# A recommendation tower (embedding look-up, pairwise products, three dense layers): the last chunk gets an order of its own, and its last gathered row another bank

## The chip, the cores and the metric

The kernel runs on one core of a Trainium2 chip. The metric is the device time of one launch in microseconds (us). TensorE multiplies matrices (PE in the rows, PEld for its weight loads), ScalarE (ACT) and VectorE (DVE) move and transform data, GpSimd (POOL) issues the indirect gathers, and SyncE (SP) issues the other DMAs. SBUF is the on-chip memory, PSUM the memory that TensorE writes, in banks of 512 float32 per partition.

## The reference, cut to what matters

```python
e = stack([tbl_f[ids[:, f]] for f in range(26)], axis=1)      # 2048 x 26 x 128
combined = concatenate([dense[:, None, :], e], axis=1)        # 2048 x 27 x 128
interactions = einsum('bnd,bmd->bnm', combined, combined)
z = concatenate([dense, interactions[:, triu_i, triu_j]], 1)  # 128 + 351
h = concatenate([z, dense], axis=1)                           # 607
h = maximum(h @ W_top1 + b_top1, 0)                           # 512
h = maximum(h @ W_top2 + b_top2, 0)                           # 256
y = h @ W_top3                                                # 2048 x 1
```

All values are float32. For each of 2048 samples 26 table rows are looked up, the 351 products of pairs among 27 vectors are made, and a small network follows.

## The kernel before, in words

The samples go in 8 chunks of 256 (chunk 0 to 7, `LAST` = 7), each of two tiles of 128. Of the 26 tables, 9 are looked up by one-hot matmuls from SBUF (`look_up`, line 446), and 17 are gathered row by row with one indirect DMA per table and tile (`gather`, lines 396 to 406, on GpSimd's queue). The gathered rows of a tile come in five batches of 4, 4, 4, 4 and 1 tables. `turn(t, b)` (lines 418 to 430) transposes batch b of tile t on TensorE into the one PSUM bank `moved`; ScalarE's `keep_batch` (827) copies it into `vectors` and counts `batch_kept`. As `moved` is one bank, every `turn` waits until the batch before it has been copied (line 426).

When the 27 vectors of a tile are there, `multiply(c, s)` (452 to 472) makes the products of step s of chunk c. A step is 64 samples, in two visits of 32 samples; each sample is one small matmul of 27 by 27, which the profile shows as two matmul records and two weight loads. Step s writes bank s of `banks`. Steps 0 and 1 are the first tile, steps 2 and 3 the second. `keep_step` (844 on ScalarE, 706 on VectorE for the very last step) copies the bank to `products`, and `write_quad` (217) writes them to a scratch tensor in HBM, three DMAs for each of four groups of partitions; one DMA loads them back as `features`, so that pairs lie on partitions. Then come `first_layer` (474, four output tiles m), `second_layer` (493, two output tiles) and `last_layer` (504), always of the chunk before: in chunk i the layers of chunk i-1 are mixed in among the products.

The order of each engine is written out by hand. On TensorE `chunk(i)` (625) does the first tile's batches and look-ups and ends with `end_of_chunk(i)` (639): first layers of the chunk before, steps 0 and 1, the five batches of the second tile, second layers, and, where there is a next chunk, steps 2 and 3 between its first look-up. For the last chunk `end_of_chunk` stops after batch 4, and `end()` (565) takes over: step 2 in two visits with halves of `second_layer(6, 1)` between, step 3 whole, and then the last chunk's own layers. These are done in two halves of 128 samples: `first_of_half(0, m)`, m 0 to 3 (line 535), `second_of_half(0)` (549), the dense part of `first_of_half(1, m)`, `last_of_half(0)` (560), the rest of `first_of_half(1, m)`, `second_of_half(1)`, `last_of_half(1)`. `last_layer(6)` stands between m = 1 and m = 2 of half 0.

On SyncE the end is `write_last(0)` (301; 12 DMAs, after step 1 is copied), `load_last(0)` (309; after these have landed), `write_last(1)` (six DMAs, after step 3 is copied; ScalarE issues the other six), `store_y(6)` (292; after chunk 6's y is copied), `load_last(1)` (after both sets of six have landed) and the stores of y. VectorE ends with `end()` (734): `keep_second` for chunk 6, `keep_step(7, 3)`, and the copies of half 0's layers with `keep_y` among them.

Of the kernel before, what the change touches and what calls it, by code (L numbers as in the profile page):

```python
# [20 lines left out]
TILE = 128  # L21
# [3 lines left out]
ALL_TILES = CHUNKS * TILES  # L25
LAST = CHUNKS - 1
# [39 lines left out]
assert CHUNK_STEPS == BANKS  # L66
KINDS = [ROWS[SHORT_] // PART_ROWS for SHORT_ in (ONE_HOT[0], ONE_HOT[-1])]
# [40 lines left out]
def build(nc, dense, ids, ids_of_field, tables, w1, b1, w2, b2, w3, out):  # L108
# [6 lines left out]
    with ExitStack() as ctx:  # L115
# [301 lines left out]
        def _(pe):  # L417
            def turn(t, b):
# [6 lines left out]
                if n:  # L425
                    pe.wait_ge(batch_kept, n)
                for m, v in enumerate(batch):
                    last = nc.tensor.transpose(moved[:, m * TILE:(m + 1) * TILE],  # L428
                                               rows[:, (t * TILE_ROWS + v) % RING, :], identity[:, :])
# [22 lines left out]
            def multiply(c, s, visits=range(VISITS)):  # L452
                for visit in visits:
                    multiply_part(c, s, visit)
# [110 lines left out]
            def end():  # L565

                every = (PAIR_TILES, *range(PAIR_TILES))
                multiply(LAST, 2, (0,))
                second_layer(LAST - 1, 1, range(0, 2))
                multiply(LAST, 2, (1,))  # L570
                second_layer(LAST - 1, 1, range(2, MTILES1))
                multiply(LAST, 3)
                first_of_half(0, 0, every)
                first_of_half(0, 1, every)
                last_layer(LAST - 1)
# [49 lines left out]
            def chunk(i):  # L625
# [11 lines left out]
                end_of_chunk(i)  # L637

            def end_of_chunk(i):
# [15 lines left out]
                if i < LAST:  # L655
                    second_layer(i - 1, 1)
                    multiply(i, 2, (0,))
                    look_up(i + 1, 0, range(0, 3))
                    multiply(i, 2, (1,))
                    look_up(i + 1, 0, range(3, 5))  # L660
                    multiply(i, 3, (0,))
                    look_up(i + 1, 0, range(5, PARTS[0]))
                    multiply(i, 3, (1,))
# [9 lines left out]
        def _(dve):  # L673
# [31 lines left out]

            def keep_step(c, s):

                first = s * STEP_GROUPS
                dve.wait_ge(step_ready, c * CHUNK_STEPS + s + 1)
# [5 lines left out]
            def keep_second():  # L715

                dve.wait_ge(second_ready, MTILES2 * LAST)
# [16 lines left out]
            def end():  # L734
                keep_second()
                keep_step(LAST, 3)
                first_of_half(0)
                first_of_half(1)
                keep_y()
# [63 lines left out]
        def _(act):  # L803
# [155 lines left out]
            def chunk(i):  # L959
# [11 lines left out]
                end_of_chunk(i)  # L971

            def end_of_chunk(i):
# [12 lines left out]
                if i < LAST:  # L986
                    keep_batch(b, 4)
                    keep_second(i - 1, 1)
                    keep_step(i, 2)
                    keep_pair(i + 1, 0)  # L990
                    keep_step(i, 3)
# [5 lines left out]
            keep_batch(ALL_TILES - 1, TILE_BATCHES - 1)  # L997
# [55 lines left out]
```

## Time and profile before

| what | us |
|---|---|
| median of 3 runs | 376.77 (374.21 to 377.0) |
| the profiled execution's own time | 376.67 |
| its span, first to last instruction | 374.9 |
| TensorE busy | 332.9 (89%) |
| GpSimd busy | 258.3 (69%) |
| VectorE busy | 208.2 (56%) |
| ScalarE busy | 188.4 (50%) |
| mean granted clock of TensorE | 0.977 of full speed |

The page gives busy time for each engine, 40 equal slices of the span (9.37 us each), the DMA queues, and the chain that ended last: from the last instruction back to what released it at each step. The timelines give start, length, and the idle time before an instruction with what ended it. "issue" is idle time for which the profile shows no awaited engine or DMA.

### The profile page before, as it was taken

Reading aid. Unit: us, or ns where it says so; the run is one execution under the profiler, and the core shown is the slowest. Engines: PE = TensorE matmul, PEld = TensorE weight load, DVE = VectorE, ACT = ScalarE, POOL = GpSimd, SP = SyncE. Lnnn points to the kernel's source line nnn. Section 1 sums busy time; section 2 is a strip of 40 time slices with the busy share of each in tenths; the row PEclk is TensorE's granted clock in tenths of the full one; section 3 lists DMA queues with packets and bytes.
Section 4 is the critical chain, followed back from the end, with each engine's and each line's share of the span. In section 5 each row is a group of like instructions: output and inputs, shape, how many; then the busy total and the mean of one; then the engine's idle time right before and its main releaser. Section 6 shows DMA issues by size and latency. Waiting matters only on the chain.

```text
span 374.9 us, 13491 instructions
## 1 busy us (share of the span) xinstructions
PE 332.9 (89%) x6048; PEld 298.3 (80%) x6048; DVE 208.2 (56%) x375; ACT 188.4 (50%) x223; POOL 258.3 (69%) x280
## 2 busy tenths in 40 slices
PE   0486767999999999999999999998999999998587
PEld 0476756998899889998899788986899779986476
DVE  3799925793189506980499128950599027900111
ACT  2697643355445664556255644555355634555102
POOL 6777777777777777777777777777777777774000
PEclk9999988699999999999999999999999999999979
DMA  7999528662237512572257223642257223521230
GB/s 174 253 237 199 186 61 242 129 221 65 53 78 177 164 52 61 123 235 53 59 110 232 69 58 83 174 157 54 56 125 234 52 57 77 136 60 44 57 59 3
DMA packets 49332, 44.24 MB, mean 118 GB/s; under 512 B 33359, under 2 KB 39094, under 8 KB 49274
## 3 DMA queue, kind: packets, MB, share of 16 engines
q1 hardware_dynamic: 39166, 25.36, 27.2%
q0 software_dynamic: 8704, 17.84, 17.9%
q8 instruction: 48, 0.79, 0.8%
q10 hardware_dynamic: 1404, 0.17, 0.4%
q14 instruction: 10, 0.08, 0.1%
HBM read 37.91 MB, written 5.44 MB: 116 GB/s over the span
## 4 chain that ended last, share of the span: by engine, by line
PE 76%; DMA 10%; POOL 4%; SPq 4%; issue 4%; ACT 3%; DVE 0%
PE banks L446 37%; PE banks L469 12%; PE moved L428 8%; PE mlp L489 8%; PE mlp L499 6%; DMA hidden<-in_tbl_dram 6%; POOL rows L403 4%; DMA rows<-in_tbl_dram,ids_sb 3%; PE banks L535 2%; SPq L252 2%; SPq L231 2%; ACT vectors L839 1%; PE mlp L511 1%; PE banks L549 1%; DMA features<-scratch 1%
## 5 line engine op out<-in xcount | busy, mean ns | idle before, releaser
L403 POOL DMA_INDIRECT rows<-in_tbl_dram,ids_sb x272 | 257.4, 946 | 83.9 <-issue 79.6
L693 DVE TENSOR_TENSOR masks<-hot_ids,row_of 125x512 fp32r<-125x512 int32 (+1 forms) x336 | 186.8, 618 | 59.5 <-PE banks L446 51.8
L446 PE MATMUL banks<-masks,high 125*128 125x256 f32 x592 | 154.3, 298 | 16.8 <-DVE low L680 16.8
L446 PE MATMUL banks<-masks,low 125*128 125x256 f32 x592 | 149.0, 289 | 0.0
L446 PEld LDWEIGHTS banks<-masks,high 125*128 125x128 f32 x592 | 117.1, 198 | 18.0 <-issue 15.1
L446 PEld LDWEIGHTS banks<-masks,low 125*128 125x128 f32 x592 | 117.4, 198 | 0.0
L839 ACT ACTIVATE vectors<-moved 128x512 f32<-128x512 f32 (+1 forms) x80 | 86.7, 1083 | 22.4 <-PE moved L428 22.4
L822 ACT ACTIVATE vectors<-banks 128x512 f32<-128x512 f32 (+1 forms) x40 | 44.3, 1108 | 70.6 <-PE banks L446 70.6
L469 PEld LDWEIGHTS banks<-vectors 128*27 128x27 f32 x4096 | 45.1, 105 | 22.1 <-issue 14.3
L469 PE MATMUL banks<-vectors 128*27 128x27 f32 x4096 | 55.0, 193 | 4.2 <-issue 2.6
L428 PE MATMUL moved<-identity,rows 128*128 128x128 f32 x272 | 45.7, 283 | 14.6 <-ACT vectors L839 6.3
L489 PE MATMUL mlp<-features,w_sb 117*128 117x256 f32 x224 | 53.0, 379 | 0.0
L852 ACT ACTIVATE products<-banks 123x432 f32<-123x432 f32 x31 | 29.4, 950 | 33.6 <-PE banks L469 33.5
L428 PEld LDWEIGHTS moved<-identity,rows 128*128 128x128 f32 x272 | 30.3, 141 | 20.2 <-issue 11.2
L489 PEld LDWEIGHTS mlp<-features,w_sb 117*128 117x128 f32 x224 | 40.4, 190 | 4.4
L702 DVE COPY vectors<-dense_sb 128x256 f32<-128x256 f32 x8 | 3.7, 459 | 60.8 <-PE banks L469 60.8
L499 PE MATMUL mlp<-hidden,w_sb 128*128 128x256 f32 x112 | 27.3, 388 | 0.0
L499 PEld LDWEIGHTS mlp<-hidden,w_sb 128*128 128x128 f32 x112 | 20.1, 190 | 2.9
L867 ACT ACTIVATE hidden<-mlp,b_sb 128x256 f32<-128x256 f32 x28 | 13.3, 474 | 14.2 <-PE mlp L489 14.0
L680 DVE TENSOR_TENSOR low<-mlp,high 125x1024 fp32r<-125x1024 f32 x9 | 11.0, 1218 | 3.5 <-ACT mlp L814 3.5
L879 ACT ACTIVATE hidden<-mlp,b_sb 128x256 f32<-128x256 f32 x13 | 6.2, 474 | 11.2 <-PE mlp L499 11.2
L766 DVE COPY features<-dense_sb 128x256 f32<-128x256 f32 x8 | 3.2, 394 | 13.5 <-PE mlp L489 13.5
(46 smaller groups left out, 67.8 us busy)
## 6 DMA issues: line engine op xcount, KB each, us to landing
hot_ids<-in_ids_of_field_dram SPq DMA_DIRECT2D x32, 256.0 KB, 4.9
rows<-in_tbl_dram,ids_sb POOLq DMA_INDIRECT x272
features<-scratch SPq DMA_DIRECT2D x7, 351.0 KB
scratch<-products SPq DMA_DIRECT2D x56, 42.2 KB
scratch<-products SPq DMA_DIRECT2D x28, 81.2 KB
w_sb<-in_tbl_dram SPq DMA_DIRECT2D x3, 448.0 KB
hot_ids<-in_ids_of_field_dram SPq DMA_DIRECT2D x8, 128.0 KB
dense_sb<-in_dense_dram SPq DMA_DIRECT2D x8, 128.0 KB, 5.0
```

Source lines behind the costliest of these rows:

```text
L403: pool.indirect_dma_start(rows[:, (tile * TILE_ROWS + v) % RING, :], None, tables[f][:, :], bass.IndirectOffsetOnAxis(ap=ids_sb[:, tile, f ...
L428: last = nc.tensor.transpose(moved[:, m * TILE:(m + 1) * TILE], rows[:, (t * TILE_ROWS + v) % RING, :], identity[:, :])
L446: last = nc.tensor.matmul(banks[:, j % BANKS, m * CHUNK:(m + 1) * CHUNK], part[:, part_of(j * PAIR + m, k), :], masks[:, mask % MASK_RING, ...
L469: last = nc.tensor.matmul(banks[to:to + VECTORS, s, g * VECTORS:(g + 1) * VECTORS], one, one, start=True, stop=True, tile_position=(0, to))
L489: last = nc.tensor.matmul(mlp[:, m % 2, 0:CHUNK], w1_sb[0:height, k, m * 128:(m + 1) * 128], features[0:height, k, :], start=(k == 0), sto ...
L499: last = nc.tensor.matmul(mlp[:, m, 0:CHUNK], w2_sb[:, k, m * 128:(m + 1) * 128], hidden1[:, k, :], start=(k == 0), stop=(k == MTILES1 - 1))
L680: done = nc.vector.tensor_tensor(low[:, p, :], whole[0:PART_ROWS, first:last, :], high[:, p, :].bitcast(fp32), ALU.subtract)
L693: nc.vector.tensor_tensor(masks[:, mask % MASK_RING, 0:size], hot_ids[0:PART_ROWS, n % ID_RING, 0:size], row_of[0:PART_ROWS, row:row + 1]. ...
L822: nc.scalar.activation(of_chunk(c, TILE_ROWS + j * PAIR, WIDTHS[j]), banks[:, j % BANKS, 0:WIDTHS[j] * CHUNK] .rearrange("d (v t s) -> d v ...
L839: nc.scalar.activation(vectors[:, at:at + TILE, batch[0]:batch[-1] + 1].rearrange("d s v -> d v s"), moved[:, 0:len(batch) * TILE].rearran ...
L852: nc.scalar.activation(products[0:PRODUCT_ROWS, ::-1, first:first + STEP_GROUPS].rearrange("p x g -> p g x"), banks[0:PRODUCT_ROWS, s, 0:S ...
L867: nc.scalar.activation(hidden1[:, m, :], mlp[:, m % 2, 0:CHUNK], ACT.Relu, bias=b1_sb[:, m:m + 1])\
```

## The change

TensorE's `end_of_chunk` is no longer called for the last chunk; `end()` holds the whole of its order. There step 1's first visit stands ahead of `first_layer(6, 2)` and its second visit right behind it, ahead of batch 2 of tile 15. `second_layer(6, 0)` is cut into halves around batch 3. Batch 4, the single last row, is transposed into bank 3 of `banks` and no longer waits for the copy of batch 3; VectorE's `keep_last_row` copies it into `vectors`. The first half of `second_layer(6, 1)` follows, then steps 2 and 3 whole and back to back, then its second half, `last_layer(6)`, and only then all four m of `first_of_half(0, m)`. ScalarE has `end_of_last()` with the matching order. VectorE ends with `keep_last_row`, `keep_step(7, 3)`, `keep_second`, `keep_y`, and then the copies of half 0; `keep_step` and `keep_second` each get one more wait, for the count before theirs. SyncE and GpSimd are not changed. No computation is added or removed.

```diff
--- before.py
+++ after.py
@@ -64,6 +64,7 @@
 
 BANKS = 4
 assert CHUNK_STEPS == BANKS
+LAST_ROW_BANK = BANKS - 1
 KINDS = [ROWS[SHORT_] // PART_ROWS for SHORT_ in (ONE_HOT[0], ONE_HOT[-1])]
 
 HIDDEN1, HIDDEN2 = 512, 256
@@ -422,10 +423,12 @@
                 n = t * TILE_BATCHES + b
                 batch = tile_batch(b)
                 pe.wait_ge(rows_loaded[t % TILES * TILE_BATCHES + b], (t // TILES + 1) * 16 * len(batch))
-                if n:
+                own = t == ALL_TILES - 1 and b == TILE_BATCHES - 1
+                if n and not own:
                     pe.wait_ge(batch_kept, n)
+                place = banks[:, LAST_ROW_BANK, :] if own else moved
                 for m, v in enumerate(batch):
-                    last = nc.tensor.transpose(moved[:, m * TILE:(m + 1) * TILE],
+                    last = nc.tensor.transpose(place[:, m * TILE:(m + 1) * TILE],
                                                rows[:, (t * TILE_ROWS + v) % RING, :], identity[:, :])
                 last.then_inc(batch_ready, 1)
 
@@ -565,14 +568,29 @@
             def end():
 
                 every = (PAIR_TILES, *range(PAIR_TILES))
-                multiply(LAST, 2, (0,))
+                b = ALL_TILES - 1
+                first_layer(LAST - 1, 0)
+                multiply(LAST, 0, (0,))
+                turn(b, 0)
+                first_layer(LAST - 1, 1)
+                multiply(LAST, 0, (1,))
+                turn(b, 1)
+                multiply(LAST, 1, (0,))
+                first_layer(LAST - 1, 2)
+                multiply(LAST, 1, (1,))
+                turn(b, 2)
+                first_layer(LAST - 1, 3)
+                second_layer(LAST - 1, 0, range(0, 2))
+                turn(b, 3)
+                second_layer(LAST - 1, 0, range(2, MTILES1))
+                turn(b, 4)
                 second_layer(LAST - 1, 1, range(0, 2))
-                multiply(LAST, 2, (1,))
+                multiply(LAST, 2)
+                multiply(LAST, 3)
                 second_layer(LAST - 1, 1, range(2, MTILES1))
-                multiply(LAST, 3)
+                last_layer(LAST - 1)
                 first_of_half(0, 0, every)
                 first_of_half(0, 1, every)
-                last_layer(LAST - 1)
                 first_of_half(0, 2, every)
                 first_of_half(0, 3, every)
                 second_of_half(0)
@@ -634,7 +652,8 @@
                 turn(a, 3)
                 look_up(i, 4)
                 turn(a, 4)
-                end_of_chunk(i)
+                if i < LAST:
+                    end_of_chunk(i)
 
             def end_of_chunk(i):
                 b = TILES * i + 1
@@ -652,15 +671,14 @@
                 multiply(i, 1, (1,))
                 second_layer(i - 1, 0)
                 turn(b, 4)
-                if i < LAST:
-                    second_layer(i - 1, 1)
-                    multiply(i, 2, (0,))
-                    look_up(i + 1, 0, range(0, 3))
-                    multiply(i, 2, (1,))
-                    look_up(i + 1, 0, range(3, 5))
-                    multiply(i, 3, (0,))
-                    look_up(i + 1, 0, range(5, PARTS[0]))
-                    multiply(i, 3, (1,))
+                second_layer(i - 1, 1)
+                multiply(i, 2, (0,))
+                look_up(i + 1, 0, range(0, 3))
+                multiply(i, 2, (1,))
+                look_up(i + 1, 0, range(3, 5))
+                multiply(i, 3, (0,))
+                look_up(i + 1, 0, range(5, PARTS[0]))
+                multiply(i, 3, (1,))
 
             pe.wait_ge(constants_made, CONSTANTS)
             first_chunk()
@@ -703,9 +721,16 @@
                                       dense_sb[:, c % 2, :].rearrange("d (v t s) -> d v t s", v=1, t=TILES))\
                     .then_inc(dense_placed, 1)
 
+            def keep_last_row():
+
+                dve.wait_ge(batch_ready, ALL_TILES * TILE_BATCHES)
+                nc.vector.tensor_copy(vectors[:, of_tile(ALL_TILES - 1):of_tile(ALL_TILES - 1) + TILE, TILE_ROWS - 1],
+                                      banks[:, LAST_ROW_BANK, 0:TILE]).then_inc(batch_kept, 1)
+
             def keep_step(c, s):
 
                 first = s * STEP_GROUPS
+                dve.wait_ge(step_kept, c * CHUNK_STEPS + s)
                 dve.wait_ge(step_ready, c * CHUNK_STEPS + s + 1)
                 nc.vector.tensor_copy(
                     products[0:PRODUCT_ROWS, ::-1, first:first + STEP_GROUPS].rearrange("p x g -> p g x"),
@@ -714,6 +739,7 @@
 
             def keep_second():
 
+                dve.wait_ge(second_kept, MTILES2 * LAST - 1)
                 dve.wait_ge(second_ready, MTILES2 * LAST)
                 dve.wait_ge(out_written, 16 * HALVES * (LAST - 1))
                 nc.vector.tensor_scalar(hidden2[:, 1, :], mlp[:, 1, 0:CHUNK], b2_sb[:, 1:2], 0.0,
@@ -732,11 +758,12 @@
                                         ALU.add, ALU.max).then_inc(first_kept, 1)
 
             def end():
+                keep_last_row()
+                keep_step(LAST, 3)
                 keep_second()
-                keep_step(LAST, 3)
+                keep_y()
                 first_of_half(0)
                 first_of_half(1)
-                keep_y()
                 first_of_half(2)
                 first_of_half(3)
                 for m in range(MTILES2):
@@ -968,7 +995,8 @@
                 keep_batch(a, 3)
                 keep_pair(i, 4)
                 keep_batch(a, 4)
-                end_of_chunk(i)
+                if i < LAST:
+                    end_of_chunk(i)
 
             def end_of_chunk(i):
                 b = TILES * i + 1
@@ -983,18 +1011,31 @@
                 keep_batch(b, 3)
                 keep_step(i, 1)
                 keep_second(i - 1, 0)
-                if i < LAST:
-                    keep_batch(b, 4)
-                    keep_second(i - 1, 1)
-                    keep_step(i, 2)
-                    keep_pair(i + 1, 0)
-                    keep_step(i, 3)
+                keep_batch(b, 4)
+                keep_second(i - 1, 1)
+                keep_step(i, 2)
+                keep_pair(i + 1, 0)
+                keep_step(i, 3)
+
+            def end_of_last():
+                b = ALL_TILES - 1
+                keep_first(LAST - 1, 0)
+                keep_batch(b, 0)
+                keep_first(LAST - 1, 1)
+                keep_step(LAST, 0)
+                keep_batch(b, 1)
+                keep_first(LAST - 1, 2)
+                keep_step(LAST, 1)
+                keep_batch(b, 2)
+                keep_first(LAST - 1, 3)
+                keep_batch(b, 3)
+                keep_second(LAST - 1, 0)
 
             first_chunk()
             second_chunk()
             for i in range(2, CHUNKS):
                 chunk(i)
-            keep_batch(ALL_TILES - 1, TILE_BATCHES - 1)
+            end_of_last()
             keep_step(LAST, 2)
             act.wait_ge(step_kept, CHUNKS * CHUNK_STEPS)
             for q in range(QUADS // 2, QUADS):
```

## Rows read from the trace of the kernel before

**Rows 1.** The page: clock by slice, instruction queue, one group of ScalarE, TensorE's counts.
```profile
PE 332.9 (89%) x6048; PEld 298.3 (80%) x6048; DVE 208.2 (56%) x375; ACT 188.4 (50%) x223; POOL 258.3 (69%) x280
...
PEclk9999988699999999999999999999999999999979
...
q8 instruction: 48, 0.79, 0.8%
```

**Rows 2.** Chain that ended last, from the last gathers on (start us, us, what).
```profile
340.73 2.57 DMA rows<-in_tbl_dram,ids_sb
...
345.24 0.75 ACT products L852
...
354.33 3.08 DMA features<-scratch
...
357.45 3.78 PE banks L535 x16
361.23 0.70 PE mlp L511 x8
361.94 1.98 PE banks L535 x16
363.92 1.79 PE banks L549 x16
...
366.60 0.53 PE moved L560 x4
367.13 1.54 PE mlp L535 x12
```

**Rows 3.** Timeline of TensorE, 331 to 354 us (start, length, instruction, [idle before]).
```profile
331.94 0.97 PE L469 MATMUL banks<-vectors 128*27 128x27 f32 x64
...
336.57 1.90 PE L489 MATMUL mlp<-features,w_sb 117*128 117x256 f32 x8
...
339.84 0.66 PE L428 MATMUL moved<-identity,rows 128*128 128x128 f32 x4 [0.64 <-DMA rows<-in_tbl_dram,ids_sb]
...
347.53 0.74 PE L469 MATMUL banks<-vectors 128*27 128x27 f32 x64 [0.83 <-ACT vectors L839]
348.20 1.13 PE L499 MATMUL mlp<-hidden,w_sb 128*128 128x256 f32 x4
349.26 0.74 PE L469 MATMUL banks<-vectors 128*27 128x27 f32 x64
...
350.99 1.07 PE L469 MATMUL banks<-vectors 128*27 128x27 f32 x105
353.21 0.36 PE L469 MATMUL banks<-vectors 128*27 128x27 f32 x23 [1.15 <-issue]
```

**Rows 4.** Timeline of ScalarE and VectorE around the last products.
```profile
344.04 1.20 ACT L839 ACTIVATE vectors<-moved 128x512 f32<-128x512 f32 x1 [1.30 <-PE moved L428]
...
351.10 0.48 DVE L719 TENSOR_SCALAR hidden<-mlp,b_sb 128x256 f32<-128x256 f32 x1 [8.45 <-PE mlp L499]
353.66 0.88 DVE L710 COPY products<-banks 123x432 f32<-123x432 f32 x1 [2.07 <-PE banks L469]
```

**Rows 5.** Timeline of SyncE's DMA queue from the last chunk's writes on.
```profile
346.00 7.16 SPq L231 DMA_DIRECT2D scratch<-products  x12
...
354.99 4.15 SPq L231 DMA_DIRECT2D scratch<-products  x6
362.40 0.54 SPq L298 DMA_DIRECT2D out_dram<-hidden  x2
363.04 0.32 SPq L317 DMA_DIRECT2D features<-scratch  x1
```

**Rows 6.** Timeline of TensorE in the first two chunks, 47 to 66 us.
```profile
47.68 0.54 PE L469 MATMUL banks<-vectors 128*27 128x27 f32 x40
49.24 1.15 PE L469 MATMUL banks<-vectors 128*27 128x27 f32 x88 [1.03 <-issue]
...
65.71 0.90 PE L428 MATMUL moved<-identity,rows 128*128 128x128 f32 x3 [2.75 <-issue]
```

## The prediction

> **What bounds the kernel now.** The change touches only the last chunk, so I read the end. The page first: TensorE is busy for 332.9 of 374.9 us, and its granted clock is full but for dips in the first 75 us and one in the slice from 356.2 to 365.5 us [rows 1]. Then the chain that ended last, from the last gathers on [rows 2]: a gather lands at 343.30, ScalarE copies a batch and then step 1, SyncE writes half 0 to the scratch tensor, the load of half 0 lands at 357.41, and from 357.45 TensorE is on the chain almost without a break. The timeline of TensorE shows four weak places ahead of that [rows 3]: 0.64 us for a gather at 339.84, 0.83 us for ScalarE's copy at 347.53, 1.15 us of "issue" in the middle of step 3, and then nothing from 353.57 to 357.45. In the last gap the clock falls: the 16 matmuls of line 535 at 357.45 take 3.78 us, the next 16 take 1.98 [rows 2], the levels of 1.2 and 2.4 GHz. SyncE's queue [rows 5] shows why the gap is there: half 0's writes start only at 346.00, because step 1's second visit stands behind batch 3 and its gather.
>
> **Part 1: half 0's writes start earlier.** Step 1's first visit now follows batch 1, so it starts at 336.57, where first_layer(6, 2) started [rows 3]. A visit takes 0.67 us where the next instruction starts at once (349.26 to 349.93) and 0.90 at 331.94; I take 0.90. The first layer is 1.83 us (336.57 to 338.40): 337.5 to 339.3. The second visit ends at 340.1. ScalarE's copy is 0.75 to 0.9 us, SyncE starts at 341.1 instead of 346.00: 4.9 earlier. From there to the landed features is 357.41 - 346.00 = 11.4 us [rows 2, 5], so 352.5. Bounds: the writes now lie beside the last gathers, for which I allow up to 1.5 us more (half of the 3.08 of the load); nothing less, since the issues alone take 7.16. Value 352.5.
>
> **Part 2: the tail of tile 15.** Batch 2 comes at 340.1, when its rows are in (339.84), and takes 0.49 to 0.6. First layer 3 ends at 342.4, ScalarE's copy of it (256 columns, as the 0.48 in rows 4) about 0.5 later. The first half of second_layer(6, 0), eight records like those at 348.20, is 1.06 us: to 344.0. Batch 3's rows landed at 343.30, so its wait is gone; it ends at 344.6. The other half goes to 345.6. Batch 4 has its rows: its gather, the last of 272, is issued one place behind the one of 340.73 (340.73 over 271 places is 1.26 us for one) and needs 2.57 as that did, so 344.6. It no longer waits for the copy of batch 3; that copy takes 1.20 [rows 4] and ends at 345.9. VectorE, idle here, copies the last row; this copy isn't in the trace; nearest are 0.48 for a copy of twice the size and 0.88 for a step, below it nothing. I take 0.4 us, so 346.3. Neither end matters: the half of second_layer(6, 1) ahead of step 2 runs from 345.8 to 346.8. Step 2 starts at 346.8, against 347.53 before. VectorE queues nothing else behind the copy until step 3.
>
> **Part 3: steps 2 and 3 back to back, where I expect a new wait.** Four visits at 0.67 would end at 349.5. But the 1.15 us of "issue" before step 3's last 23 records has a twin in chunk 0: a step that follows a whole step stops for 1.03 us after 40 records [rows 6]. Elsewhere longer matmuls part the visits. The page has an instruction queue of 48 packets for 12,096 TensorE instructions, 252 each; 0.79 MB in 48 is 16.4 KB each [rows 1]. So I read these as instruction fetches, one block of about 256 instructions ahead of use. Counting back 256 from the stop at 352.06 (step 3 had issued 105 records, so 210 with the weight loads; 8 for the half second layer; 38 more) gives a point 0.47 us into the visit of 349.26, at 349.73. The next block was usable at 353.21, 3.48 us later. Now the same count for both orders, from first_layer(6, 0) on (a visit is 128 instructions, four first layers 64, the batches 34, half a second layer 8). Before, 898 stand ahead of step 3, so the stop came after 1108 and the boundary before it is at 852. After, 64 + 512 + 34 + 16 + 8 = 634 stand ahead of step 2 and 890 ahead of step 3, so both boundaries fall 218 instructions into these steps, give or take a few waits that may count too. The first is at 346.8 + 1.14 = 347.95, and the block behind the second is usable at 351.4. TensorE reaches that one 256 instructions on, at 349.3, and stops for 2.1 us. Step 3 ends at 351.75. Bounds of this wait: 0, if the fetch runs further ahead than I read; 2.75, the longest "issue" stop of the trace [rows 6]. Value 2.1, between but nearest to the row of the same place.
>
> The Trainium skill speaks against this term ("Runtime: NRT & Kernel Launch", Instruction fetch mechanics): blocks of 256 instructions are fetched while the one before runs, and the fetch is said to be hidden. By that rule step 3 would end at 349.5 and the sum would be rival A's. The stops above disagree with "hidden" for these small matmuls, so I keep the wait.
>
> **Part 4: from step 3 to the layers of half 0.** VectorE copies step 3 from 351.8 to 352.7 (0.88 each) [rows 4]; it was 353.66 to 354.54, so 1.85 earlier. The new wait for step 2's copy costs nothing: ScalarE has it before 350. TensorE does the other half of second_layer(6, 1), 351.7 to 352.7; keep_second is 0.48, to 353.25; last_layer(6) is 0.70, to 354.0. In the new order all of half 0's layers stand behind it, so they start at 354.0, not at 352.5 when the features are in. This is the new bound: 3.45 us ahead of 357.45. Two more terms: last_layer's 0.70 no longer stands inside the stretch, and the clock, if it stays up over the stop, makes the first 16 matmuls 1.98 instead of 3.78, so 1.80. Then 354.0 + 3.96 + 1.79 + 0.90 (363.92 + 1.79 to 366.60) + 0.53 = 361.2, where the rest of half 1 starts; it was 367.13.
>
> **Part 5: is half 1 there?** Step 3 is copied at 352.7; SyncE's six writes begin 0.45 later and take 4.15 [rows 5], to 357.3; store_y(6) is ready and takes 0.6; the writes land by about 358.3. Before, load_last(1) waited behind store_y, whose y came only at 362.4. The load's price is 3.08 at most (half 0's, beside other writes); so it lands by 361.4, 0.2 after it is needed, or before it. Value 0; bound 0.5. The rest is as before, 374.9 - 367.13 = 7.77, to 368.95.
>
> **Sum.** 3.45 + 0.70 + 1.80 = 5.95 us less: 376.67 - 5.95 = 370.7. The profiled execution's time stands 0.1 below the median of the runs, so I leave it.
>
> **Rivals.** A, no stop in steps 2 and 3. For it: in other chunks step 2 and 3 with look-ups between show no stop. Against: both whole steps that follow 128 or more small matmuls do. Then TensorE is free at 351.7 and half 0 starts when the features land, 352.5 (1.5 us earlier than 354.0): 369.2.
>
> B, the clock falls in the new stop. For it: a stop of 2.75 us in chunk 1 and the gap of 3.88 at the end each came with a dip of the clock [rows 1, 6]. Against: 1.03 us in chunk 0 did not, and mine lies between. Price: the half second layer (1.06) and last_layer (0.70) at half speed add about 1.5 by the ratio 3.78 to 1.98, and the 1.80 is in part lost: 0.3 to 1.8, I take 0.6. So 2.1 more: 372.8. The Trainium skill ("TensorE: Matmul & The Clock Gate", HAM oscillation) says that waits between bursts of matmuls bring the throttle back, which would make B the case; the chunk 0 row shows that not every wait does.
>
> C, slower than before: the fetch that steps 2 and 3 wait for is held up by half 0's scratch writes, which the new order lets run beside it. Place: the stop in step 3. Every microsecond more is one on the path through last_layer. With the clock down (B) the kernel is no better than before once the fetch takes 3.48 + 3.9 = 7.4 us, and 377.5 at 8.1. For it: the stop of 2.75 us shows that a fetch can come much later. Against: before, the fetch of 3.48 lay beside the same writes.
>
> D, the half-0 writes are slowed by gathers by so much that the features land after 354.0 and gate again. It would take more than 1.5 us; then 371 to 372, inside the range.
>
> **How the numbers follow.** The forecast 370.7 has 0.40, A 0.16, B 0.29, C 0.05, D 0.07, and a slower end that I haven't named 0.03. A measurement of this kernel can tell about 1% from no change, and 1% less than 376.77 is 373.0. The forecast, A and D are faster by more than that; B is so in two cases of three, else within; C is half within, half slower. Faster 0.82, within 1% 0.12, slower 0.06. The range is 368.0 to 374.2: below A by 1.2 (the unknown 0.90 of a visit, and a shorter landing than 11.4), above B by 1.4 (a clock that stays down longer).
>
> **What would show it.** Right: SyncE's 12 writes start near 341.1; TensorE waits for no copy ahead of step 2; an "issue" gap near 2 us late in step 3; step 3's copy on VectorE near 351.8; half 0's layers start right behind last_layer(6), 32 matmul records in 4 us; the chain leads through step 3, not through SyncE's first writes. Wrong: no such gap (A); a granted clock of 0.50 between 350 and 356 (B); a gap of over 5 us (C); TensorE waiting for half 0's load after last_layer (D), or for half 1's load for over 0.5 us ahead of the last 24 matmuls of line 535.

## The result, and the profile after

The changed kernel takes 371.62 us (median of 6 runs, 370.89 to 372.16) against 376.88 us (median of 6, 374.03 to 378.36): 5.26 us less, and 5.95 were forecast, 370.7 us. The ratio of the two is 0.9895 with a 95% interval of 0.9853 to 0.9936; this ratio, like every one below, leaves out the slowest runs. The forecast's own ratio, 370.7 to 376.77, is 0.984, just below that interval. So the kernel is faster by about 1%, beyond the noise, and by less than was forecast. The kernel before spreads wide enough to explain the difference: 29 later runs of it gave 372.38 to 379.75, 11 of them below 374.6 and 18 above 375.3, while the changed kernel's six lie within 1.3 us. What sets this spread is open. The profiled execution of the kernel before, at 376.67, is one of the longer ones, and the working below explains the two profiled executions. Against the 11 shorter runs of the kernel before the change gains 0.8 to 3 us, against the 18 longer ones 3.7 us and more.

Spans first. In the execution after, the gathers ran 0.79 us later: the last is issued at 342.77 instead of 341.98. I count from this issue to the end of the span: 374.9 - 341.98 = 32.92 us before, 369.8 - 342.77 = 27.03 us after, 5.89 less. I call this stretch the tail. In the kernel before TensorE waits in it for a gather (1.12 us at 343.34). In the changed kernel it no longer does: its last wait for a gather ends at 301.42, and from there to the end the chain holds TensorE's work, the stop, and short stretches of ScalarE and VectorE. Counted from that wait (300.74 and 301.42) the difference is much the same, 5.78 us. The tail is thus a fair measure only where TensorE loses nothing between that wait and the last gather, and the experiments have to be looked at for that.

The chain that ended last, after the change (start us, us, what), answers to [rows 2]:

```profile
343.40 0.48 ACT hidden L894
...
347.34 2.15 PE banks L472 x139
349.48 1.96 issue
351.44 0.44 PE banks L472 x18
351.88 2.02 PE mlp L502 x4
...
353.98 0.49 DVE hidden L745
354.48 0.04 issue
354.52 0.57 PE mlp L514 x4
355.10 3.77 PE banks L538 x32
358.87 1.79 PE banks L552 x16
...
361.55 0.53 PE moved L563 x4
362.07 1.53 PE mlp L538 x12
```

SyncE's writes and the load of half 0 have left the chain; it now runs through steps 2 and 3, with the stop that was forecast between them, through second_layer(6, 1), keep_second and last_layer(6). Half 0's layers start at 355.10, 12.33 us after the last gather's issue (15.47 before), and their 32 matmuls need 3.77 us; before, 6.47 us passed from 357.45 to 363.92. That is 3.14 and 2.70 of the 5.89; the rest is alike.

The timelines of TensorE, then SyncE's queue, answer to [rows 3, 5]:

```profile
346.20 0.27 PE L431 MATMUL banks<-identity,rows 128*128 128x128 f32 x1
...
347.27 2.21 PE L472 MATMUL banks<-vectors 128*27 128x27 f32 x238
351.44 0.44 PE L472 MATMUL banks<-vectors 128*27 128x27 f32 x18 [1.96 <-issue]
351.81 2.07 PE L502 MATMUL mlp<-hidden,w_sb 128*128 128x256 f32 x4
353.82 1.28 PE L514 MATMUL mlp<-hidden,w_sb 128*1 128x128 f32 x8
355.03 3.84 PE L538 MATMUL banks<-features,w_sb 128*128 128x128 f32 x32
```

```profile
342.09 5.50 SPq L232 DMA_DIRECT2D scratch<-products  x12
348.76 0.30 SPq L318 DMA_DIRECT2D features<-scratch  x1
352.91 4.26 SPq L232 DMA_DIRECT2D scratch<-products  x6
...
359.01 0.32 SPq L318 DMA_DIRECT2D features<-scratch  x1
```

and VectorE's copies of the last row and of step 3:

```profile
346.51 0.41 DVE L727 COPY vectors<-banks 128x128 f32<-128x128 f32 x1 [2.67 <-PE banks L431]
351.99 0.90 DVE L735 COPY products<-banks 123x432 f32<-123x432 f32 x1 [5.07 <-PE banks L472]
```

The stop comes behind record 238 of the 256 of steps 2 and 3; 237 was forecast, and 1.96 us against 2.1. The half second layer at 351.81 needs 2.07 us where four such records took 1.13 before [rows 3]: the clock fell right behind the stop. The stretches of the same execution (us, busy time and count of TensorE, its weight loads, VectorE, ScalarE and GpSimd, then granted clock, DMA share, GB/s):

```profile
350.00:351.00 1.00, 0.00 (x0) 0.00 (x0) 0.00 (x0) 0.00 (x0) 0.00 (x0) 1.00 0.52 148
351.00:352.00 1.00, 0.56 (x19) 0.50 (x20) 0.01 (x1) 0.00 (x0) 0.00 (x0) 0.77 0.00 1
352.00:353.00 1.00, 1.00 (x3) 0.82 (x4) 0.89 (x1) 0.00 (x0) 0.00 (x0) 0.50 0.00 0
...
354.00:355.00 1.00, 0.89 (x8) 0.09 (x4) 0.47 (x1) 0.00 (x0) 0.00 (x0) 0.53 0.71 76
355.00:356.00 1.00, 1.00 (x10) 0.97 (x9) 0.38 (x1) 0.00 (x0) 0.00 (x0) 1.00 0.81 113
```

The mean of 0.77 puts the fall from 2.4 to 1.2 GHz at about 351.56, 0.1 us behind the end of the stop, and the 0.53 puts the return at about 354.94, just as half 0's layers began.

### The profile page after: what moved, and what is told of

The parts are those of the page before. It is cut to its first block, busy times and chain, and to the rows that moved or that the text cites. A ratio compares the mean times of both kernels' runs of the same rounds, so it can differ in the third digit from the quotient of the medians.

```text
span 369.8 us, 13491 instructions
## 1 busy us (share of the span) xinstructions
PE 331.2 (90%) x6048; PEld 295.2 (80%) x6048; DVE 208.4 (56%) x376; ACT 188.2 (51%) x222; POOL 259.1 (70%) x280
## 4 chain that ended last, share of the span: by engine, by line
PE 78%; DMA 8%; POOL 4%; issue 4%; SPq 2%; ACT 2%; DVE 0%; DVEq 0%
PE banks L449 37%; PE banks L472 13%; PE mlp L492 8%; PE moved L431 8%; PE mlp L502 7%; DMA hidden<-in_tbl_dram 6%; POOL rows L404 4%; DMA rows<-in_tbl_dram,ids_sb 3%; SPq L253 2%; PE banks L538 1%; PE mlp L514 1%; PE banks L552 1%; ACT vectors L866 1%; ACT vectors L849 1%; PE mlp L538 1%
## 5 line engine op out<-in xcount | busy, mean ns | idle before, releaser
L449 PE MATMUL banks<-masks,high 125*128 125x256 f32 x592 | 152.4, 296 | 16.7 <-DVE low L698 16.7
L449 PE MATMUL banks<-masks,low 125*128 125x256 f32 x592 | 147.2, 287 | 0.0
L449 PEld LDWEIGHTS banks<-masks,high 125*128 125x128 f32 x592 | 115.6, 195 | 17.7 <-issue 14.6
L449 PEld LDWEIGHTS banks<-masks,low 125*128 125x128 f32 x592 | 115.9, 196 | 0.0
L472 PE MATMUL banks<-vectors 128*27 128x27 f32 x4096 | 56.3, 193 | 4.7 <-issue 3.7
L502 PE MATMUL mlp<-hidden,w_sb 128*128 128x256 f32 x112 | 28.2, 396 | 0.6 <-ACT hidden L894 0.6
```

The lines of the kernel that those rows point to most:

```text
L449: last = nc.tensor.matmul(banks[:, j % BANKS, m * CHUNK:(m + 1) * CHUNK], part[:, part_of(j * PAIR + m, k), :], masks[:, mask % MASK_RING, ...
L472: last = nc.tensor.matmul(banks[to:to + VECTORS, s, g * VECTORS:(g + 1) * VECTORS], one, one, start=True, stop=True, tile_position=(0, to))
L502: last = nc.tensor.matmul(mlp[:, m, 0:CHUNK], w2_sb[:, k, m * 128:(m + 1) * 128], hidden1[:, k, :], start=(k == 0), stop=(k == MTILES1 - 1))
```

## The experiments

Ten kernels ran, two of them a second time for more times and another trace (the labels that end in `_timed`). Each is compared by its tail (last gather's issue to the end of the profiled span); where a kernel ran only once, its time is given in brackets. One execution is weak evidence for anything below about 1 us: the same program gave tails of 27.28 and 26.18 us in two executions (`between_pad53`, below).

### Is the stop a fetch of instructions?

`pad32` and `pad55` add this at TensorE's start, with N = 32 and 55:

```diff
             pe.wait_ge(constants_made, CONSTANTS)
+            for _ in range(N):
+                nc.tensor.matmul(moved[0:VECTORS, 0:VECTORS], identity[:, 0:VECTORS],
+                                 identity[:, 0:VECTORS], start=True, stop=True, tile_position=(0, 0))
```

> The changed kernel with 32 extra small matmuls of TensorE right at its start, while it waits for the first table (128 instructions more ahead of everything; their results are overwritten). Fetch theory (the stop in step 3 is a wait for the next block of 256 instructions): every block boundary now falls 128 instructions, 64 matmul records, earlier in the program, so the stop moves from behind record 238 of the 256 of steps 2 and 3 to behind record 174, and stays about 2.0 us long, since each block still takes about 3.2 us from the crossing of the boundary before. Step 3 ends as late as before (about 4.5 us after step 2's start). Rival (the stop belongs to the place: bank 3 just freed by the copy of the last row, or to step 3 itself): it stays behind record 238. Third view, a slow spell of the DMA queues at that time: it stays at its time, whatever record that is.

> The same with 55 extra matmuls, 220 instructions. Fetch theory: the boundary falls between steps 2 and 3, so the stop lies behind record 128 of 256, and the boundary before it lies at the very start of step 2. If TensorE's sequencer reads ahead of what it executes, that block can be asked for while the half second layer still runs, up to 1 us earlier; then the stop is 1 to 2 us and step 3 ends up to 1 us earlier, else as before. Rival of place: still behind record 238.

TensorE's timeline of `pad32`:

```profile
348.26 1.68 PE L472 MATMUL banks<-vectors 128*27 128x27 f32 x174
352.19 0.89 PE L472 MATMUL banks<-vectors 128*27 128x27 f32 x82 [2.24 <-issue]
...
364.29 2.88 PE L538 MATMUL mlp<-features,w_sb 117*128 117x128 f32 x12 [2.15 <-DMA features<-scratch]
```

and of `pad55`:

```profile
346.93 2.64 PE L472 MATMUL banks<-vectors 128*27 128x27 f32 x256
351.76 1.13 PE L502 MATMUL mlp<-hidden,w_sb 128*128 128x256 f32 x4 [2.18 <-issue]
...
354.05 5.20 PE L538 MATMUL banks<-features,w_sb 128*128 128x128 f32 x32
```

128 instructions put in some 350 us earlier moved the stop by exactly 64 records, from 238 to 174. Nothing about bank 3, step 3 or the moment explains that: the stop lies at a block boundary, every 256 instructions. `pad55` was half wrong: the boundary between the steps (record 128) is crossed without a stop, and the stop is at the next, behind record 256. The DMA queue for instructions shows why. It moves one packet (0.02 MB) for each block: in the changed kernel at 349.0, 0.5 us ahead of the stop and 2.4 us ahead of its end. In `pad55` the packets pass at 345.8 and 349.4. The first is the block behind record 128, moved 1.1 us before step 2, at whose start the boundary before it lies: TensorE's sequencer reads ahead of the engine. So step 3 ended 2.64 us after step 2's start instead of 4.6.

The tails are 31.26 us for `pad32` (375.46) and 27.83 for `pad55` (371.96), neither below the 27.03 of the change. `pad55` lost what it had gained to the clock, which fell at about 353.5, 1.8 us behind its stop: half 0's 32 matmuls took 5.20 us instead of 3.84. In `pad32` three things add up. The clock fell behind a wait of 1.76 us for a gather at 301.23, so that eight records of a second layer took 3.67 us at 302.72 instead of the 1.99 of the changed kernel. TensorE waited for nothing that could have absorbed this, and step 2 began 5.82 us after the last gather instead of 4.50. This 1.3 us has nothing to do with the steps. Then the path I had bounded at 0.5 us, half 1's features, came 2.15 us late, and the clock fell at the end of that wait: the 12 matmuls behind it show 2.88 us where they take 1.60. SyncE had issued its last write at about 358 but could issue the load only at 361.42, as the writes' semaphores came late. Why they did is open.

### The last row's bank

`undo_bank`: the last row goes to `moved` again and ScalarE copies it. `undo_bank_pad8` is the same with N = 8 in the loop above.

```diff
-                own = t == ALL_TILES - 1 and b == TILE_BATCHES - 1
+                own = False
...
-                keep_last_row()
...
                 keep_batch(b, 3)
+                keep_batch(b, 4)
```

> The changed kernel with the last gathered row transposed into the old bank again and copied by ScalarE. Theory: its transpose waits for ScalarE's copy of batch 3 (ends 0.5 us after the transpose started in the changed kernel), everything behind it on TensorE moves by that, and since the tail runs on TensorE from there to the end, the end comes 0.5 us later, counted from the last gather's issue (27.0 us in the changed kernel, so 27.5). Rival: nothing, because the half second layer and the stop in step 3 cover it (27.0).

> undo_bank with 8 extra small matmuls at the start (32 instructions), so that the block boundaries lie elsewhere. If the second stop of undo_bank (1.68 us behind record 109 of steps 2 and 3) came only from where its boundaries lie against its waits, it goes; one stop of about 2 us remains behind record 221 or 222, and from the last gather's issue to the end it takes 27.5 us. If the bank itself costs what undo_bank showed (30.3 us), both stops stay, 16 records earlier.

> The kernel of undo_bank, timed, to tell chance from place. If the second stop of 1.68 us comes from where this program's block boundaries lie, every execution has it: 374 to 375, ratio to the kernel before 0.994. If it was a chance of one execution, the median is 372.1 (the changed kernel plus 0.5) and some runs are higher.

TensorE in `undo_bank`:

```profile
346.58 0.30 PE L431 MATMUL moved<-identity,rows 128*128 128x128 f32 x1 [0.49 <-ACT vectors L865]
...
347.68 1.10 PE L472 MATMUL banks<-vectors 128*27 128x27 f32 x109
350.46 1.28 PE L472 MATMUL banks<-vectors 128*27 128x27 f32 x128 [1.68 <-issue]
354.46 0.35 PE L472 MATMUL banks<-vectors 128*27 128x27 f32 x19 [2.72 <-issue]
```

and in `undo_bank_pad8`:

```profile
346.10 0.30 PE L431 MATMUL moved<-identity,rows 128*128 128x128 f32 x1 [0.50 <-ACT vectors L868]
...
347.20 2.06 PE L472 MATMUL banks<-vectors 128*27 128x27 f32 x221
351.52 0.46 PE L472 MATMUL banks<-vectors 128*27 128x27 f32 x35 [2.26 <-issue]
```

The wait for ScalarE's copy is 0.49 and 0.50 us, as expected. But `undo_bank` has two stops, 128 records apart, and a tail of 30.34 us; with 32 more instructions at the start there is one stop, at record 221, and the tail is 27.16 (370.94). What the bank gives is best read at step 2's start, which lies 5.22 and 5.26 us after the last gather here and 4.50 in the changed kernel: 0.7 us. How much of it reaches the end isn't shown, since the clock stayed up in `undo_bank_pad8` and fell in the changed kernel. Of the 3.2 us between the two tails without the bank, 1.68 are the first stop, 0.5 the longer second one (2.72 against 2.26) and 1.0 the clock, which fell only in `undo_bank`. The first stop is a block that came late: its packet passes at 348.0, and the one before at 337.6, while the changed kernel has one at 341.6 for the same boundary. Why it was asked for so late is open. Timed, `undo_bank` takes 373.9 us, from 371.44 to 375.66 in 10 runs, three of them below 372. The execution traced there (374.78) has both stops again, 1.40 and 2.72 us, and a tail of 30.94. So the second stop is no single accident. Whether the three short runs had one stop only isn't shown, as none of them was traced. Its ratio to the kernel before is 0.9954 (0.9906 to 1.0003).

### Step 1's place

```diff
-                multiply(LAST, 1, (0,))
                 first_layer(LAST - 1, 2)
-                multiply(LAST, 1, (1,))
+                multiply(LAST, 1, (0,))
                 turn(b, 2)
                 first_layer(LAST - 1, 3)
-                second_layer(LAST - 1, 0, range(0, 2))
                 turn(b, 3)
-                second_layer(LAST - 1, 0, range(2, MTILES1))
+                multiply(LAST, 1, (1,))
+                second_layer(LAST - 1, 0)
```

> The changed kernel with step 1 where it was in the kernel before: its first visit behind first_layer(6, 2), its second behind batch 3, second_layer(6, 0) whole behind that, and ScalarE's order to match. Theory: half 0's writes start about 4.5 us later than 342.1, its features land at about 357 to 358 and gate its layers, which start 2 to 3 us later than 355.03; the clock is down in the gap and costs up to 1.8 more where it wasn't already. From the last gather's issue to the end 29.5 to 32 us instead of 27.0. Rival (the path through step 3 and last_layer is what counts, the early writes are idle cover): 27.0 to 27.5.

(ScalarE's copy of step 1 moves behind that of batch 3 to match.) The tail is 29.1 us, 2.1 more (372.88). TensorE waits at two places where it didn't in the changed kernel, for batch 3's gather, and, as SyncE starts half 0's writes only at 346.02, for their features:

```profile
343.36 0.66 PE L431 MATMUL moved<-identity,rows 128*128 128x128 f32 x4 [1.78 <-DMA rows<-in_tbl_dram,ids_sb]
...
356.33 3.84 PE L538 MATMUL banks<-features,w_sb 128*128 128x128 f32 x32 [0.67 <-DMA features<-scratch]
```

This is less than the range I gave, and only a part of it is the reason I gave. Step 2 begins 5.51 us after the last gather instead of 4.50: 1.0 us is lost because no work of step 1 is left to fill the wait for batch 3's gather. The late features cost 0.67, since the path through step 3 stands only that far behind them, and the stop was 0.27 us longer. So the early writes by themselves are worth about 0.7 us here, and the place of step 1's visits ahead of the gather about 1.0.

### last_layer's place

```diff
-                last_layer(LAST - 1)
                 first_of_half(0, 0, every)
                 first_of_half(0, 1, every)
+                last_layer(LAST - 1)
```

(and `keep_y` behind the first two copies on VectorE.)

> The changed kernel with last_layer(6) and keep_y back between m = 1 and m = 2 of half 0. My prediction counted 0.70 us for the move. Theory on that term: last_layer stands on TensorE's path in both places, so its own 0.7 us is no gain; in the changed kernel it even adds VectorE's keep_second (0.6 us of waiting), which would be covered here. So half 0's first matmul starts right behind the half second layer, about 1.2 to 1.9 us earlier than 355.03, second_of_half(0) starts about 0.6 us earlier than in the changed kernel, and the end is 0.6 us earlier (26.4 us from the last gather's issue, instead of 27.0). Rival (the move is worth 0.7): 27.7.

```profile
351.51 0.35 PE L472 MATMUL banks<-vectors 128*27 128x27 f32 x18 [2.52 <-issue]
...
352.94 3.40 PE L538 MATMUL banks<-features,w_sb 128*128 128x128 f32 x16
...
358.69 1.95 PE L552 MATMUL banks<-hidden,w_sb 128*128 128x128 f32 x16
```

The tail is 27.6 us (371.57), by the number near the rival. But its stop was 0.56 us longer (2.52 us), which no move of last_layer explains. From the stop's end to second_of_half(0) it takes 351.51 to 358.69, 7.18 us; in the changed kernel 351.44 to 358.70, 7.26. In both some 1.3 to 1.6 us of it is low clock, which here fell on half 0's first matmuls (3.40 us for 16, 2.05 at the full clock) instead of on the half second layer and last_layer. So in these two executions the move is worth nothing, in either direction: both of my numbers were wrong.

### The clock, by itself

`before_filled` puts matmuls of no use into the gap of the kernel before:

```diff
                 multiply(LAST, 3)
+                for _ in range(4):
+                    nc.tensor.matmul(moved[:, :], identity[:, :], w1_sb[:, PAIR_TILES, :], start=True, stop=True)
```

> The kernel before the change, with four idle matmuls of 512 columns (16 instructions; their result in the free bank is overwritten) behind step 3, in the gap of 3.88 us in which TensorE waited for half 0's features. Clock theory: they keep the engine busy for about 3.5 us, the clock stays at its full level, the first 16 matmuls of half 0 take 1.98 us instead of 3.78, and the end comes 1.8 us earlier (ratio to the kernel before 0.995). This is the term of 1.80 in my prediction, measured by itself. Rival (the clock falls in any case, or these 16 are slow for another reason, such as freshly landed features): 3.78 stays, ratio 1.000.

```profile
353.62 3.70 PE L574 MATMUL moved<-w_sb,identity 128*128 128x512 f32 x8
357.66 2.05 PE L535 MATMUL banks<-features,w_sb 128*128 128x128 f32 x16 [0.34 <-DMA features<-scratch]
```

In the profile all happens as expected: 2.05 us for the 16 matmuls that took 3.78, the granted clock 1.00 throughout, and a tail of 373.2 - 342.12 = 31.08, 1.84 less than 32.92. In time the median goes from 376.48 (29 runs) to 374.97 (12 runs), 1.5 less, yet the ratio is 1.0005 (0.997 to 1.0039), which is no gain. The 12 runs lie from 374.13 to 376.22; of the 29 without the idle matmuls 9 are below that and 16 above. So 1.8 us is the clock's share of the profiled execution; that every execution of the kernel before pays it isn't shown.

### Shorter stops

`layer_between` has the half second layer between the steps and `keep_second` ahead of `keep_step(7, 3)`; `between_pad53` adds N = 53 at the start; `filled` has N = 51 and two idle matmuls of 512 columns behind step 3.

```diff
                 multiply(LAST, 2)
-                multiply(LAST, 3)
                 second_layer(LAST - 1, 1, range(2, MTILES1))
+                multiply(LAST, 3)
                 last_layer(LAST - 1)
```

> The changed kernel with the last half of second_layer(6, 1) between steps 2 and 3, and keep_second ahead of keep_step(7, 3) on VectorE. Fetch theory: the stop moves 8 instructions, to behind record 234, and is about 1 us instead of 1.96, since the half layer (1.0 us, 8 instructions) runs while the block comes; step 3 ends at the same 4.5 us after step 2's start; half 0's layers start right behind step 3 and last_layer, about 2.5 us earlier than 355.03 with the clock up. Then half 1's features are what comes last: TensorE waits 1 to 2 us for them, and the end is 0.5 to 1 us earlier (26.0 to 26.5 us from the last gather). Rival (the stop comes from steps back to back, as such): no stop.

> layer_between with 53 extra small matmuls at the start (212 instructions), so that boundaries lie about 8 instructions into step 2, behind the half layer, and at step 3's end. Fetch theory: no stop inside steps 2 and 3, step 3 ends about 3.9 us after step 2's start instead of 4.5, and the stop stands behind step 3 (1 to 2 us). Half 1's writes start 0.6 us or more earlier. From the last gather's issue to the end 25.5 to 26.5 us.

> The kernel of between_pad53, timed. One look gave 371.2; the change itself 371.6. Theory: its half 0 starts about 1.3 us earlier than the changed kernel's but with the clock down, so 370.5 to 371.5, ratio to the kernel before 0.986. If its clock is up in some executions, those are near 369.5.

> between_pad53 with 51 instead of 53 extra small matmuls at the start, and two idle matmuls of 512 columns behind step 3, ahead of the block boundary, so that TensorE works through most of the stop there. Clock theory: the granted clock stays at 1.00, half 0's 32 matmuls take 3.8 us instead of 5.46, half 1's rest starts 1.5 us earlier than there if its features are in (they landed just about then), and from the last gather's issue to the end 25.6 to 26.3 us (changed kernel 27.0, between_pad53 27.3). Time 369.5 to 370.5, ratio to the kernel before 0.983. Rival (the clock falls after any such stretch of small matmuls): as between_pad53, 371.2.

TensorE in `layer_between`:

```profile
350.54 1.09 PE L472 MATMUL banks<-vectors 128*27 128x27 f32 x106
352.41 0.33 PE L472 MATMUL banks<-vectors 128*27 128x27 f32 x19 [0.78 <-issue]
...
362.07 1.63 PE L538 MATMUL mlp<-features,w_sb 117*128 117x128 f32 x12 [1.84 <-DMA features<-scratch]
```

The stop moves to record 234 and shrinks to 0.78 us, as the fetch theory has it, and the clock stays up. Yet the tail is 28.94 us (373.25). As in `pad32`, 1.3 us of it was lost at 302.81, where the clock had fallen behind a wait for a gather (1.78 us), and isn't of this edit. Half 0's layers start 1.6 us nearer to the last gather than in the changed kernel, 2.9 us nearer to step 2's start, but TensorE then waits 1.84 us for half 1's features, and 1.4 us behind that wait the clock falls. Counted from step 2's start the end still comes 0.6 us later than in the changed kernel (23.12 against 22.53 us). `between_pad53` has no stop inside the steps, as expected, and one of 2.29 us behind them. Its two profiled executions differ mainly in what the clock made of that:

```profile
352.48 0.60 PE L514 MATMUL mlp<-hidden,w_sb 128*1 128x128 f32 x8 [2.29 <-issue]
353.02 5.46 PE L538 MATMUL banks<-features,w_sb 128*128 128x128 f32 x32
```

and timed

```profile
352.17 0.60 PE L514 MATMUL mlp<-hidden,w_sb 128*1 128x128 f32 x8 [1.95 <-issue]
352.71 3.84 PE L538 MATMUL banks<-features,w_sb 128*128 128x128 f32 x32
```

with tails of 27.28 and 26.18 us. In the first the clock fell at about 354.0, 1.5 us behind the stop; in the second it stayed up, and 0.85 of the 1.6 us saved went into a wait for half 1's features. Timed it is 370.35 us (368.83 to 373.24, 4 runs), ratio 0.9885 (0.9797 to 0.9973), which can't be told from the change's 0.9895. Three of the four runs are below all six of the changed kernel and one is above them, too few to say more. `filled` kept the clock at 1.00 and did its 32 matmuls in 3.84, but with its boundaries 8 instructions further on, the read-ahead came too late (packet at 348.0 instead of 345.6): a stop of 0.72 us behind record 4 of step 3, one of 0.58 behind the idle matmuls. Its tail is 27.07 and its time 371.55 (370.66 to 373.13), ratio 0.991 (0.9871 to 0.9949): no better than the change. No version tried clearly beats the changed kernel.

## Why the prediction was right

The forecast of the tail held (5.95 forecast, 5.89 measured), and of its mechanism the earlier writes, the stop and its place, and the new path through step 3. One part of the mechanism failed, the clock, and that the number still fits is partly luck. Times of after are given less the 0.79 us by which its gathers ran late.

**Part 1** held where it starts and was pessimistic behind: SyncE began at 341.3 (341.1 forecast), and its writes and load were done about 8.8 us later, not 11.4. That changed nothing, as the features weren't what half 0 waited for. `undo_step1` shows what the part is worth: 0.7 us for the early writes, and 1.0 us for filling the wait for batch 3's gather, which belongs to part 2.

**Part 2** held: batches 3 and 4 wait for nothing, and step 2 starts at 346.5 (346.8). The one wait ahead of it, 0.56 us for ScalarE's copy of first layer 3, was in the working. VectorE's copy of the last row took 0.41 us (0.4).

**Part 3** is the step on which the forecast stood, and the runs bear it out: the boundary is where the count put it, and moves with the count. The block came 3.2 us after the crossing of the boundary before (3.48). What I didn't see is the reading ahead, which the packets of `pad55` show: a block can come in time although its boundary is crossed only later, and in `undo_bank` it came late with almost the same code. What decides this is open. The Trainium skill ("Runtime: NRT & Kernel Launch", Instruction fetch mechanics) has the block of 256 instructions right, and it is borne out by the 64 records; that the fetch is hidden is not, by 1.96 us here.

**Part 4** landed at 354.3 (354.0) by two errors that cancelled. Step 3 ended at 351.1 (351.75), because step 2 began 0.3 us early and the block came 0.3 us sooner than assumed. But the condition "the clock, if it stays up over the stop" failed: it fell 0.1 us behind the stop, at about 350.8, and was back at about 354.2. So the half second layer took 2.02 us on the chain instead of 1.0. From its end to half 0's layers it was 1.20 us, with keep_second and last_layer, against 1.3 in the working; at the full clock it would have been less, as the last four records of last_layer show 0.57 us here and all eight 0.60 in `before_filled`. A granted clock of 0.50 between 350 and 356 was the sign I had named for rival B, so B's mechanism occurred. The Trainium skill ("TensorE: Matmul & The Clock Gate", HAM oscillation) says that waits between bursts bring the throttle back; its example has waits of 3 to 5 us, longer than the 1.96 us of this stop. This trace agrees with it, while `undo_bank_pad8`, with a stop of 2.26 us, shows no fall. Of B's price of 2.1 us only 1.0 to 1.3 (an estimate, from the 1.0 of the half second layer and up to 0.3 of last_layer) was paid: its second part, slow layers of half 0, was not, with 3.77 us for all 32 (3.96). That the clock came back at that moment was luck; in `pad55`, `undo_last` and the first `between_pad53` it was down under these layers. The two terms behind it, 1.80 and 0.70, came out as 2.70 (6.47 less 3.77). `before_filled` measures the clock's at 1.84. The 0.70 is real inside the stretch but is paid ahead of it; it was in my start at 354.0, so the sum was right and only the name of a gain was not. `undo_last` agrees: moving last_layer back changed nothing.

**Part 5** held in the changed kernel (load issued at 359.01, first used at 362.07 without a wait), but it is the next bound: in `pad32`, `layer_between` and the timed `between_pad53` TensorE waits 2.15, 1.84 and 0.85 us there.

Sum: 5.95 forecast, 5.89 in the tails of two executions, 5.26 between the medians. Rival A fell with the stop. Rival C, a fetch held up for so long that the kernel is slower, did not occur in the changed kernel; `undo_bank` shows a late block, but nothing ties it to the scratch writes. D did not occur.

## What to carry to other kernels

Before putting small matmuls back to back, count instructions: here 512 of them were issued in 2.64 us, and each block of 256 needs 3.2 to 3.5 us. Long matmuls with few instructions placed between them make such a stop shorter: four records between the steps took it from 1.96 to 0.78 us in `layer_between`, though the kernel as a whole was no faster. Where an edit moves instructions in a stream like this, compare it with a version padded at the start, and with a second execution, before putting a microsecond down to the edit itself.

## What the runs showed of the hardware that I had not expected

A stop of TensorE of about 2 us brings the clock down in some executions and not in others: stops of 1.96, 2.18, 2.23, 2.29 and 2.52 us were followed by a granted clock of 0.50, from 0.1 to 1.8 us behind their end; stops of 1.95, 2.24 and 2.26 us were not, and the same program (`between_pad53`) showed both. The waits for a gather at about 301 us are the same: behind 1.74, 1.76 and 1.78 us it fell in `before_filled`, `pad32` and `layer_between`, while other executions kept it behind waits of 1.71 to 1.78 us. A program with 128 instructions more in its first microseconds ended 4.2 us later (tails of 27.03 and 31.26), but 1.3 of this is that fall at 301 us, and with one execution of each the rest isn't shown to be the instructions' either. And the semaphores of the last writes to HBM came up to 3.5 us after the last was issued (357.92 to 361.42 in `pad32`), against 1.8 in the changed kernel (357.17 to 359.01).
